# Wavelet attention and a mixture of experts on one core: the shared expert moved from GpSimd to VectorE, a convolution band moved to TensorE

## The reference

```python
x = x + attn(layernorm(x))     # wavelet attention, below
x = x + ffn(layernorm(x))      # 16 experts and one shared expert

# attn: two levels of a 4-tap depthwise convolution with stride 2
l, h = dwconv(low, h_filter)[:, ::2], dwconv(low, g_filter)[:, ::2]   # h is the high band, kept
low = linear_attention(low, 16)            # on the twice halved rows
low = dwconv(repeat(low, 2), h_synth) + dwconv(repeat(h, 2), g_synth) # per level, backwards
return layer_norm(x + low, norm_gamma, norm_beta)

# ffn: each expert takes the 256 rows with its highest scores (of 2048)
scores = sigmoid(h @ gate_w.T)
topk_score, topk_ids = top_k(scores.T, 256)
eo = silu(xin @ gw + gb) * (xin @ up_w + up_b) @ down_w + down_b      # per expert, 128 -> 512 -> 128
out = zeros.at[topk_ids].add(eo * topk_score)
shared = (silu(x @ sh_gate_w) * (x @ sh_up_w)) @ sh_down_w            # all rows, 128 -> 256 -> 128
return out + shared
```

## Time and profile before

| | us |
|---|---|
| runs | 258.89, 257.4, 254.8 (median 257.4) |
| profiled execution, its own time | 252.19 |
| its span | 250.4 |

### The profile page before, as it was taken

The page is one execution under the profiler, slowest core; times in us unless marked ns, Lnnn a source line. Parts: engine busy times, 40 slices in busy tenths (PEclk is TensorE's granted clock), DMA queues, the critical chain, the costliest instruction groups (busy, mean ns, idle before and its releaser), DMA issues.

```text
span 250.4 us, 3543 instructions
## 1 busy us (share of the span) xinstructions
PE 199.3 (80%) x1268; PEld 168.7 (67%) x1268; DVE 137.2 (55%) x371; ACT 82.6 (33%) x188; POOL 132.6 (53%) x125
## 2 busy tenths in 40 slices
PE   7289659999699866877695999999999988889300
PEld 7165557999599433545553789999999878878200
DVE  3779994659923697987482244444444444445100
ACT  2474100135746111122040243444434333334200
POOL 7419930035410021253558868888888888656561
PEclk9957988999955899999799799999999999999955
DMA  6999990000001800000102232333333333322231
GB/s 214 416 414 420 411 387 18 0 3 1 3 1 54 302 3 0 0 29 16 42 0 77 62 89 33 48 45 44 42 39 46 45 47 45 44 24 22 21 29 13
DMA packets 11585, 22.20 MB, mean 89 GB/s; under 512 B 1456, under 2 KB 8752, under 8 KB 11440
## 3 DMA queue, kind: packets, MB, share of 16 engines
q1 hardware_dynamic: 5936, 17.52, 18.1%
q0 software_dynamic: 5632, 4.46, 13.8%
HBM read 17.65 MB, written 4.33 MB: 88 GB/s over the span
## 4 chain that ended last, share of the span: by engine, by line
PE 36%; DVE 24%; DMA 14%; POOL 12%; issue 7%; ACT 3%; POOLq 1%; SPq 0%; DVEq 0%
DMA out_dram<-area,rows 11%; POOL out_dram L445 7%; PE bank L1187 5%; PE bank L1188 5%; PE bank L1171 4%; PE bank L1040 3%; PE bank L926 3%; DVE area L761 3%; DMA x_tok<-in_x_dram 3%; DVE stats L594 2%; PE bank L1019 2%; PE bank L891 2%; POOL hT L433 2%; DVE hT L659 2%; DVE hT L650 2%
## 5 line engine op out<-in xcount | busy, mean ns | idle before, releaser
L445 POOL DMA_INDIRECT out_dram<-area,rows x32 | 50.7, 1585 | 19.4 <-DMA out_dram<-area,rows 10.0
L876 DVE SCALAR_TENSOR_TENSOR area<-bank,consts,sgate 128x256 f32<-128x256 f32 x64 | 30.8, 482 | 36.6 <-ACT sgate L573 36.5
L573 ACT ACTIVATE sgate<-bank,consts 128x256 f32<-128x256 f32 x64 | 30.0, 468 | 48.0 <-PE bank L1188 48.0
L1187 PE MATMUL bank<-area,wT 128*128 128x256 f32 x128 | 40.3, 397 | 3.8 <-issue 2.8
L1171 PEld LDWEIGHTS bank<-wT,area 128*128 128x128 f32 x256 | 38.3, 191 | 3.2
L1188 PE MATMUL bank<-area,wT 128*128 128x256 f32 x128 | 39.0, 387 | 0.0
L1171 PE MATMUL bank<-wT,area 128*128 128x128 f32 x256 | 38.6, 275 | 0.0
L433 POOL DMA_INDIRECT hT<-h_rows,rows x32 | 31.5, 983 | 9.5 <-issue 8.9
L421 POOL TENSOR_TENSOR sh_hid<-sh_up,sgate 128x512 f32<-128x512 f32 x8 | 12.7, 1592 | 42.7 <-ACT sh_up L563 37.8
L383 POOL TENSOR_TENSOR rstd<-var_eps,half_pow 128x4 f32<-128x4 f32 (+1 forms) x10 | 12.5, 1250 | 31.7 <-DVE var_eps L599 31.7
L1188 PEld LDWEIGHTS bank<-area,wT 128*128 128x128 f32 x128 | 25.0, 195 | 3.5
(11 more groups left out here) (161 smaller groups left out, 280.0 us busy)
## 6 DMA issues: line engine op xcount, KB each, us to landing
wT<-in_weights_dram SPq DMA_DIRECT2D x16, 768.0 KB, 17.7
h_rows<-hrow SPq DMA_DIRECT2D x2, 576.0 KB, 4.1
x_tok<-in_x_dram SPq DMA_DIRECT2D x2, 512.0 KB, 5.2
x_tok<-in_down_b_dram SPq DMA_DIRECT2D x1, 1024.0 KB, 7.1
out_dram<-x SPq DMA_DIRECT2D x4, 256.0 KB, 2.1
hT<-h_rows,rows POOLq DMA_INDIRECT x32, 2.6
out_dram<-area,rows POOLq DMA_INDIRECT x32, 3.4
sh_wT<-in_shared_dram SPq DMA_DIRECT2D x1, 384.0 KB, 7.3
```

Of the source, the lines that this page charges most:

```text
L445: pool.indirect_dma_start(out=out_rows, in_=eo[:, e % 2, c, :], in_offset=None, out_offset=bass.IndirectOffsetOnAxis(ap=rows[:, g, c, k:k ...
L573: act.activation(sgate_e[:, q % SGB, :], up_bank(q)[:, CAP:2 * CAP], ACT.Silu, bias=biasT[:, 1, j, e:e + 1]).then_inc(s_sil, 1)
L876: dve.scalar_tensor_tensor(hidden[:, e % 2, j, :], up_bank(q)[:, 0:CAP], biasT[:, 0, j, e:e + 1], sgate_e[:, q % SGB, :], ALU.add, ALU.mul ...
L1187: pe.matmul(up_bank(q)[:, 0:CAP], wT[:, e, 0, j, :], xselT[:, e % 2, :], start=True, stop=True)
```

## The change

It does six things.

1. The high band of sequence 1 is made by four matmuls into bank 5 (`analyse_high(1)`), behind `add_xn(1)` and ahead of `synth2_high(0)`, and ScalarE copies it. GpSimd's seven operations go. Its addition of beta is cut into four, one per group, and waits for the second level's high band (`s_h2`).
2. The shared expert's product and its addition to `x1` go from GpSimd to VectorE and read the PSUM banks directly. ScalarE's copies to `sh_up` and `sh_down` go. The eight products and the four additions are put into the rounds (`meanwhile`), and into the tables' stage.
3. On TensorE the shared expert starts earlier: group 0's `up` parts stand in the router's end, the others in the rounds, and the last `fall` behind the first table.
4. The warming matmuls of the last group (4) and behind the router (3 and 3) are dropped.
5. The rows' second group is made inside the first expert's work; `turn_x(0)` waits for the first group alone.
6. In the last router group, the `up` parts of group 0 stand ahead of `features_T(3)`.

```diff
@@ GpSimd @@
             pool.wait_ge(s_const, 16)
-            pool.wait_ge(s_xp, 4)
-            acc, part = h1p[:, 1, 1:N1 + 1], sgate[:, 0, :]
-            for k, (r, o) in enumerate(PHASE):
-                dst = part if k else acc
-                link(pool.tensor_tensor(dst, xp[:, r, 1, o:o + N1], taps[:, 4 + k:5 + k].to_broadcast([P, N1]), ALU.mult))
-                if k:
-                    ins = pool.tensor_tensor(acc, acc, part, ALU.add)
...
             pool.wait_ge(s_xnv, NB)
             pool.wait_ge(s_xna, NB)
-            pool.tensor_tensor(x_tok[:, :, :], x_tok[:, :, :],
-                               beta_bc.unsqueeze(1).to_broadcast([P, NT, C]), ALU.add).then_inc(s_xb, 1)
+            pool.wait_ge(s_h2, 1)
+            for g in range(LAST + 1):
+                pool.tensor_tensor(x_tok[:, group(g), :], x_tok[:, group(g), :],
+                                   beta_bc.unsqueeze(1).to_broadcast([P, 4, C]), ALU.add).then_inc(s_xb, 1)
...
-            for n in range(LAST + 1):
-                for t in range(SHT):
-                    pool.wait_ge(s_shsil, SHT * n + t + 1)
-                    pool.wait_ge(s_shupe, SHT * n + t + 1)
...
-                    pool.tensor_tensor(sh_hid[:, n % 2, t, :], sh_up[:, t, :], sgate[:, t, :], ALU.mult).then_inc(s_shhid, 1)
-                if n:
-                    shared_add(n - 1)
...
             for e in range(GBUF - 1):
                 gather(e)
-                if e == 3:
-                    shared_add(LAST)
@@ ScalarE @@
-            act.wait_ge(s_h1, 1)
-            act.copy(h1p[:, 0, 1:N1 + 1], bank[4][:, :]).then_inc(s_h1a, 1)
+            for b in range(NB):
+                act.wait_ge(s_h1, b + 1)
+                act.copy(h1p[:, b, 1:N1 + 1], bank[4 + b][:, :]).then_inc(s_h1a, 1)
...
                     act.activation(sgate[:, t, :], bank[t][:, :], ACT.Silu).then_inc(s_shsil, 1)
-                    act.wait_ge(s_shu, SHT * n + t + 1)
-                    act.copy(sh_up[:, t, :], bank[2 + t][:, :]).then_inc(s_shupe, 1)
-                if n:
-                    keep_down(n - 1)
-            keep_down(LAST)
+            act.wait_ge(s_shhid, SHT * (LAST + 1))
@@ VectorE @@
+            def shared_hidden(n, t):
+
+                dve.wait_ge(s_shsil, SHT * n + t + 1)
+                dve.wait_ge(s_shu, SHT * n + t + 1)
+                if n >= 2:
+                    dve.wait_ge(s_shout, n - 1)
+                dve.tensor_tensor(sh_hid[:, n % 2, t, :], bank[2 + t][:, :], sgate[:, t, :], ALU.mult).then_inc(s_shhid, 1)
+
+            def shared_add(n):
+
+                dve.wait_ge(s_shout, n + 1)
+                x1_n = x1[:, group(n), :].rearrange("p i c -> p (i c)")
+                dve.tensor_tensor(x1_n, bank[4][:, :], x1_n, ALU.add).then_inc(s_base, 1)
+
+            def meanwhile(r):
+
+                if r in (1, 2):
+                    shared_hidden(0, r - 1)
+                elif r in (3, 4):
+                    shared_hidden(1, r - 3)
+                elif r == 5:
+                    shared_add(0)
+                elif r in (6, 7):
+                    shared_hidden(2, r - 6)
+                elif r == 8:
+                    shared_add(1)
+                elif r == 9:
+                    shared_hidden(3, 0)
...
+                meanwhile(r)
                 dve.wait_ge(s_tot, r + 1)
...
             link(dve.tensor_scalar(above_no[:, :], bank[6][:, 0:E], -UNSET, None, ALU.add))
+            shared_hidden(3, 1)
             dve.wait_ge(s_pos, 1)
...
+            shared_add(2)
             own_expert(0)
             keep_table(0)
             slot_rows(0)
             link(one_hot(one_lo, 1, 1))
             times_token(1)
             one_hot(one_hi, 0, 1).then_inc(s_hot, 1)
-            own_expert(1)
-            keep_table(1)
-            slot_rows(1)
+            shared_add(3)
...
+            keep_x(0)
+            own_expert(1)
             dve.wait_ge(s_db_in, 16)
-            keep_x(0)
             for q in range(E * FT):
                 e, j = divmod(q, FT)
+                if q == 1:
+                    keep_table(1)
+                if q == 3:
+                    slot_rows(1)
@@ TensorE @@
+            def analyse_high(b):
+                pe.wait_ge(s_xp, 2 * b + 2)
+                for k, (r, o) in enumerate(PHASE):
+                    last = pe.matmul(bank[4 + b][:, :], diag[:, k, :], xp[:, r, b, o:o + N1], start=(k == 0), stop=(k == 3))
+                last.then_inc(s_h1, 1)
+
+            analyse_high(0)
...
             add_xn(0)
             add_xn(1)
+            analyse_high(1)
             synth2_high(0)
...
-            WARM_T = (8, 8, 2, 4)
-            WARM_L, WARM_C = 3, 3
-            for g in range(LAST + 1):
+            WARM_T = (8, 8, 2)
+            for g in range(LAST):
                 pe.wait_ge(s_x1b, g + 1)
                 stay_warm(WARM_T[g], bank[5])
                 features_T(g)
                 if g:
                     router(g - 1)
-            last = router(LAST)
-            last.then_inc(s_logit, 1)
-            stay_warm(WARM_L, bank[6])
+            pe.wait_ge(s_shw, 16)
+            pe.wait_ge(s_aff, LAST + 1)
+            up(0, 0, 1)
+            features_T(LAST)
+            router(LAST - 1)
+            up(0, 2)
+            router(LAST).then_inc(s_logit, 1)
+            up(0, 3)
...
-            stay_warm(WARM_C, bank[6])
...
-                if r < 4:
-                    up(0, r)
-                elif r < 8:
-                    up(1, r - 4)
-                    if r > 4:
-                        fall(0, r - 5)
-                elif r == 8:
-                    up(2, 0)
-                    fall(0, 3)
-                else:
-                    up(2, 1)
+                if r == 0:
+                    up(1, 0)
+                elif r == 1:
+                    up(1, 2)
+                elif r == 2:
+                    up(1, 1)
+                elif r == 3:
+                    up(1, 3)
+                    fall(0, 0, 1)
+                elif r == 4:
+                    fall(0, 2, 3)
+                    up(2, 0)
+                elif r == 5:
+                    up(2, 1, 2)
+                elif r == 6:
+                    up(2, 3)
+                    fall(1, 0, 1)
+                elif r == 7:
+                    fall(1, 2, 3)
+                    up(3, 0)
+                elif r == 8:
+                    up(3, 1, 2)
+                else:
+                    up(3, 3)
+                    fall(2, 0, 1)
...
             positions()
-            fall(1, 0)
-            up(2, 2)
-            fall(1, 1, 2)
-            up(2, 3)
-            fall(1, 3)
+            fall(2, 2, 3)
...
             table(0)
-            fall(2, 0)
             turn_table(0)
             spread(0)
-            up(3, 0, 1)
-            fall(2, 1)
-            up(3, 2, 3)
-            fall(2, 2, 3)
+            fall(3, 0, 1, 2, 3)
             table(1)
-            pe.wait_ge(s_rows, 1)
-            turn_table(1)
-            spread(1)
...
                 if e == 0:
-                    pe.wait_ge(s_rows, 2)
+                    pe.wait_ge(s_rows, 1)
...
+                if q == 0:
+                    turn_table(1)
+                if q == 2:
+                    spread(1)
```

91 lines of the change are left out of this document (32 added, 59 removed).

## The result

The changed kernel takes **243.17 us** (median of four runs, 242.11 to 244.14) where the kernel before, run beside it, takes 256.1 (252.0 to 258.89). The ratio is 0.964, 95% interval 0.959 to 0.969: faster, 3.8 us under the forecast and 0.7 us above the lower end of the range. The profiled execution took 242.11 us, span 240.4. Executions of one kernel differ with the granted clock: the kernel before, run beside the later experiments, took 244.57 us at a mean clock of 0.957, 250.57 at 0.921 and 258.73 at 0.885, and the four runs of the changed kernel had 0.913 to 0.922. By these numbers, an estimate, 7 to 8 of the 12.9 us between the medians stand at equal clock.

A forecast was written before the change was run, and what follows sets the result against it. GpSimd's scatters were taken to bound the end, after a TensorE-VectorE path. Terms -4.0 - 0.4 + 0.6 - 1.1 - 5.5 = -10.4 gave 241.8 us profiled; with 5.2 for the median, 247.0 us, range 242.5 to 252.0.

The forecast's parts named there:

- The end belongs to GpSimd's scatters, so count to the first scatter: Kernel's tail: first scatter to end stays 100.1 us, so the change is worth what it moves the first scatter.
- Head, -4.0: Start to the attention's numerator: 2.3 us from an earlier second turn, 1.7 from the clock staying up; bounds -4.0 and +1.1.
- Router's end, -0.4: Second router group to first count: +0.9 us up to the scores, -1.3 behind them; bounds -2.8 and +2.5.
- The rival that the clock stays at half up to the scores: Router's end: waits for features break the dense stretch, +2.4 us, 249.4 in all; 15%.
- Rounds, +0.6: Ten search rounds: VectorE's added products and additions cost +2.2 us, -1.6 is given back; bounds 0 and +3.
- The 1.6 us given back: Search rounds: three rounds lengthened by 0.52 us each beside GpSimd's work were to lose that extra time.
- To R, -1.1: Rounds' end to the first group's row numbers: second one-hot takes 1.23 us, not 2.29, with GpSimd idle.
- R to the first scatter, -5.5: From the first group's row numbers to the first scatter: 19.2 us instead of 24.7; bounds -6.3 and -3.
- the rival at 15%: Experts' start: first gathers and one-hots hold each other, TensorE starts later, +2.3 us, 249.3 in all; 15%.
- Waiting for ScalarE and not for a gather: Expected sign at the experts' start: the first scatter, at about 140 us, waits for ScalarE.
- The rule on ports: VectorE and GpSimd share a port pair; two SBUF inputs collide, one does not, so products from PSUM are harmless.
- the three signs of being wrong: Rounds more than 3.2 us apart, the first gather held, or a changed time from first scatter to end.

The follow-up runs named there:

- e8: Changed kernel with the second group's one-hots, table, turn and row numbers moved in among the products of experts 0 to 3; 245.41 us, ratio 0.989.
- e10: Changed kernel with the high band of the second sequence computed on GpSimd again, without TensorE's four matmuls and ScalarE's copy; 241.91 us, ratio 0.969.
- e4: Changed kernel with the four up matmuls of the shared expert's first group behind the router's last group; 242.9 us.
- e2: Changed kernel with 2 one-column copies added to ScalarE's list ahead of its wait for the experts; 244.47 us, one run.
- e11: Changed kernel with seven of the eight shared-expert products computed twice on VectorE, in seven of the ten rounds; 242.74 us, one run.
- e5: Changed kernel with three experts gathered ahead instead of five, so 8 gathers in a row instead of 12; 239.18 us, ratio 0.960.
- e3: Changed kernel with GpSimd's first gather waiting for VectorE's three one-hot operations of the second group; 243.19 us, one run.

## Why the prediction was right or wrong

*The end belongs to GpSimd's scatters, so count to the first scatter*: right for the order, wrong that the tail is untouched. It was 100.06 us, now 103.88, and 100.5 to 104.1 in the other kernels with 12 gathers, e8 apart. Part of it is the second scatter pair, 7.29 us behind the first instead of 6.40 in the profiles where it waits for ScalarE; part are longer waits for landings near the end (3.79 us at 215.06), which no run here explains.

*Head, -4.0*: right in size, and in naming GpSimd's long additions as what VectorE waited beside. The first band's records ran at the same clock in both profiles, so this is no luck of the clock. The edit that did it is the one to the beta additions (e10). The price of the matmuls, 3.44 us, was met to the hundredth.

*Router's end, -0.4*: the profiled execution shows -3.6, outside the bound of -2.8, but only because the clock stayed up in it, which is luck: the sum had it fall there as before. Where it fell, as it had before the change, the stretch is 42.8 to 43.0 (e4 apart) against 43.35: -0.4. There its two parts are met too: numerator to scores 40.08 in e2 against 39.11 before, +1.0 for the +0.9 of the sum, and scores to first counts 2.90 against 4.24, -1.3. The clock came back behind the first two `up` parts there, as in the sum. What I missed is that there are two cases, 3.2 us apart, with the same instructions ahead. The rival that the clock stays at half up to the scores came in none of these profiles.

*Rounds, +0.6*: mis-sized, and of the wrong sign; they took 1.3 us less. I charged 0.69 + 0.03 - 0.48 = 0.24 us for each product, its full duration and a gap. VectorE starts the next instruction 0.60 us after its start, and base to reading was 0.74 us before and is 0.19 + 0.60 = 0.79 now: 0.05 a round. The 1.6 us given back were right; e11 confirms the price.

*To R, -1.1*: right, -0.9.

*R to the first scatter, -5.5*: too good by 2.2. TensorE started at R + 7.16 instead of 6.8, because the first gather began 0.92 us behind R and not 0.2, and the second was held (the rival at 15%, half right: only the gather gives way, and costs 0.67 us of waiting for the transfer, not 2.3). The rest is the hold: 13.04 us to the start of the weighing instead of 11.1 (the 11.8 of the sum is its end), or 9.73 without the hold at full clock (e5). So the hold cost 3.3 us, of which 1.4 stood in the sum, as the slower matmuls of the kernel before. "Waiting for ScalarE and not for a gather" came true, with another cause than I meant.

*The rule on ports.* The trace gave 0.96 us for the second gather alone and 1.85 beside the one-hots, whose inputs are both in SBUF. The Trainium skill, "SBUF — State Buffer", section "Who interferes with whom", infers that such an instruction leaves the making of descriptors alone. By e3 and e8 (2.00 us for the 11th gather) the gather as a whole is held. A gather also reads its row numbers from SBUF, and the same section lets two readers of SBUF collide, so either the inference fails or that reading is what is held; no run separates the two. The section exempts a VectorE instruction with one SBUF input only outside what it calls the 2-port perf modes, a condition that the prediction leaves out; the tensor_scalar that was held for 4.62 us has one SBUF input.

The sum for the profiled execution was 241.8 us and it took 242.11, because errors cancel, which is luck: rounds -1.9 and the clock -3.2 against +6.0 for the way to the first scatter and the tail. Of the three signs of being wrong that the prediction names, two came: a gather was held, and the time from the first scatter to the end changed. The median is 3.8 us under the forecast, since I had added the 5.2 us by which the median before stood above its profiled execution; after the change that distance is 1.1. So the range held the result with its mechanism right in the head, and in the tables, and with three later steps wrong: the price of a product, the way from R to the first scatter, and the tail.

## What to carry to other kernels

Price an instruction put into an engine's stream by the distance between starts of its like (0.60 us here), not by its duration (0.68). When a source of transfers is let loose earlier, the tail is not "unchanged": ask how many transfers will then be queued in a row while the consumers run, and try fewer ahead (12 to 8 brought 3.3 us here up to the first weighing). And when a change has several items, undo each alone before crediting it: the head's gain came with the edit to the beta additions, half of one item, and not with the matmuls that the item is named for. Compare stages at like clock too: 3.2 us of the profile's gain were a clock that fell in one execution and not in the other.
